# The recurrence's TensorE program written out chunk by chunk, padded to 1280 instructions each, with nine bf16 products ahead of it

## The reference, cut to what matters

```python
def step(carry, xs):
    W_in, W_out = carry
    q_t, k_t, v_t, lr_t = xs
    k_h = softmax(einsum('blhd,bDhd->blhD', k_t, W_in)) * lr_t[..., 1:]
    q_h = softmax(einsum('blhd,bDhd->blhD', q_t, W_in))
    qk = einsum('bqhD,bkhD->bhqk', q_h, k_h) * mask
    o_t = einsum('bqhD,bDhd->bqhd', q_h, W_out) + einsum('bhqk,bkhd->bqhd', qk, v_t)
    W_out = W_out + einsum('bnhD,bnhd->bDhd', k_h, v_t)
    for _ in range(2):
        g_out = -attn(W_in, k_t, v_t)
        g_in = -attn(W_out, v_t, k_t)
        W_in = W_in - lr_in * g_in
        W_out = W_out - lr_out * g_out
    return ((W_in, W_out), o_t)
_, o = lax.scan(step, (W_in0, W_out0), (qc, kc, vc, lrc))
```

## Time and profile before

| what | value |
|---|---|
| median of 3 runs | 2547.16 us |
| the profiled execution's own time | 2548.93 us |
| its span | 2547.1 us |
| TensorE busy | 2187.3 us (86%), 32499 products |
| VectorE, ScalarE, GpSimd busy | 1596.5, 1565.8, 1102.3 us |
| stage B, 434 to 1226 us: mean granted TensorE clock | 0.81 of full |
| stage C, from 1226 us: the same | 0.97 |

### The profile page before, as it was taken

The page is one execution under the profiler, slowest core; times in us unless marked ns, Lnnn a source line. Parts: engine busy times, 40 slices in busy tenths (PEclk is TensorE's granted clock), DMA queues, the critical chain, the costliest instruction groups (busy, mean ns, idle before and its releaser), DMA issues.

```text
span 2547.1 us, 88423 instructions
## 1 busy us (share of the span) xinstructions
PE 2187.3 (86%) x32499; PEld 1393.0 (55%) x32499; DVE 1596.5 (63%) x3901; ACT 1565.8 (61%) x4121; POOL 1102.3 (43%) x1221
## 2 busy tenths in 40 slices
PE   7999995877877777777389999999999999999898
PEld 3555542554544545455246566565665656647466
DVE  6888885665665665666247467474774747647465
ACT  6888873665665665666248456484564846648464
POOL 1221222665666666666523333444233442334323
PEclk9999997787897887878699999999999999999999
DMA  6555556222322323221321231212313122130120
GB/s 203 166 171 156 162 160 163 53 65 64 84 66 65 69 67 78 52 67 38 95 79 42 74 75 43 74 34 74 75 43 87 28 72 69 43 97 4 40 50 18
DMA packets 387244, 201.52 MB, mean 79 GB/s; under 512 B 257376, under 2 KB 372704, under 8 KB 386800
## 3 DMA queue, kind: packets, MB, share of 16 engines
q1 hardware_dynamic: 386800, 195.65, 28.9%
HBM read 101.67 MB, written 69.27 MB: 67 GB/s over the span
## 4 chain that ended last, share of the span: by engine, by line
PE 48%; DVE 16%; issue 15%; ACT 15%; POOL 2%; SPq 2%; DMA 1%; DVEq 1%; ACTq 1%; POOLq 0%
PE psum L1035 11%; ACT arena L1554 8%; DVE arena L1846 6%; PE psum L1128 4%; PE psum L899 4%; PE psum L887 3%; PE psum L894 3%; PE psum L1087 3%; PE psum L1095 3%; ACT arena L1353 3%; PE psum L907 2%; PE psum L1201 2%; PE psum L1067 2%; PE psum L1164 2%; DVE arena L1855 1%
## 5 line engine op out<-in xcount | busy, mean ns | idle before, releaser
L1780 POOL TENSOR_TENSOR arena<-arena 128x400 f32<-128x400 f32 x256 | 218.8, 855 | 483.3 <-DVE arena L2205 483.3
L1353 ACT ACTIVATE arena<-psum,scan_sb 64x128 f32<-64x128 f32 x1152 | 311.5, 362 | 122.4 <-PE psum L964 60.4
L1554 ACT ACTIVATE arena<-psum,arena 128x100 f32<-128x100 f32 x1024 | 271.0, 368 | 6.8 <-DVE arena L2197 6.7
L1846 DVE SCALAR_TENSOR_TENSOR arena<-psum,taps_sb,arena 128x511 f32<-128x511 f32 (+2 forms) x288 | 212.3, 747 | 54.4 <-ACT arena L1253 47.6
L808 PE MATMUL psum<-arena,w_in_sb 128*128 128x512 f32 x512 | 229.7, 597 | 1.0 <-ACT arena L1246 1.0
L1925 DVE TENSOR_TENSOR arena<-psum,scan_sb 64x512 f32<-64x512 f32 x290 | 190.2, 674 | 31.7 <-PE psum L995 18.3
L899 PE MATMUL psum<-arena,scan_sb 128*128 128x512 f32 x264 | 194.7, 829 | 3.8 <-issue 2.0
L894 PE MATMUL psum<-arena 128*32 128x17 f32 x10240 | 140.3, 196 | 64.5 <-issue 39.6
L1596 POOL TENSOR_TENSOR arena<-arena 128x512 f32<-128x512 f32 x64 | 80.8, 1275 | 263.9 <-ACT arena L1279 263.9
L1673 POOL TENSOR_TENSOR arena<-arena 128x512 f32<-128x512 f32 x128 | 133.9, 1068 | 131.7 <-ACT arena L1408 118.6
L2197 DVE TENSOR_REDUCE arena<-psum 128x4 f32<-128x400 f32 x256 | 146.4, 573 | 59.1 <-PE psum L1151 49.1
(11 more groups left out here) (223 smaller groups left out, 4706.9 us busy)
## 6 DMA issues: line engine op xcount, KB each, us to landing
arena<-arena SPq DMA_DIRECT2D x144, 128.0 KB
arena<-x SPq DMA_DIRECT2D x32, 512.0 KB, 3.9
arena<-gates_d SPq DMA_DIRECT2D x112, 128.0 KB, 4.0
v_rows_d<-arena SPq DMA_DIRECT2D x64, 136.0 KB
k_rows_d<-arena SPq DMA_DIRECT2D x64, 136.0 KB
arena<-k_rows_d SPq DMA_DIRECT2D x128, 68.0 KB, 2.0
arena<-v_rows_d SPq DMA_DIRECT2D x128, 68.0 KB, 2.1
v_d<-arena SPq DMA_DIRECT2D x32, 256.0 KB, 4.3
```

The costliest lines, as they stand in the source:

```text
L1353: ins = act.activation(dst.rearrange("p (t x a) -> p t x a", x=PP, a=INNER)[upper, :, x], src.rearrange("p (t a) -> p t a", a=INNER)[upper ...
L1554: act.activation(c_soft[s][:, f % 2, u], sc, ACT.Exp, bias=c_max[s][:, u:u + 1]).then_inc(c_act.mark(f"exp{s}{f}u{u}"), 1)
L1780: pool.tensor_tensor(soft, soft, c_rec[s].unsqueeze(2).broadcast_to([P, 4, KEYS]), ALU.mult).then_inc(c_pool.mark(f"prob{s}{f}"), 1)
L1846: ins = dve.scalar_tensor_tensor(out=a_acc[:, t, j:TOK], in0=bank[2 + t][:, 0:TOK - j], scalar=taps_sb[:, t % KT, col:col + 1], in1=a_acc[ ...
```

## The change

TensorE's loop over rounds becomes a Python loop, so that all 32 chunks stand in its instruction list and all its wait counts are constants. The other engines keep their loops. In each chunk, six `hold` instructions are put behind the transpose `tb1` and ahead of the waits for `pb0`, and one behind `pb1` and ahead of the wait for `wi1`. Ahead of the wait for the start state, nine products of 128x128 by 128x400 in bf16 are put, which write a bank that the later code overwrites.

```diff
             mm.then_inc(st_pe.mark("rates"), 1)
             phase_a_done(pe)
 
+            def keep_busy(count):
+
+                for _ in range(count):
+                    pe.matmul(bank[4][:, 0:2 * KT * KEYS], identb[:], mask_sb[:, 0:2].rearrange("p a b -> p (a b)"), start=True, stop=True)
+
+            keep_busy(9)
             pe.wait_ge(st_dve.sem, st_dve.at(0, "in"))
...
-            with pe.Fori(0, ROUNDS) as n:
+            for n in range(ROUNDS):
...
                     pe.transpose(bank[1][:, 3 * P:4 * P], e_b[:, 1], ident[:]).then_inc(mine.mark("tb1"), 1)
+                    for _ in range(6):
+                        hold(pe)
                     pe.wait_ge(dve.sem, dve.at(c, "xb0"))
...
                     updates(grid(bank[0][:, 0:PP * ROW17], ROW17), pb_in[1], k_rows[i % 2], every).then_inc(mine.mark("pb1"), 1)
+                    hold(pe)
                     pe.wait_ge(dve.sem, dve.at(c, "wi1"))
```

## The result

The changed kernel takes 2502.81 us (median of 4 runs, 2501.26 to 2503.51) against 2547.27 us of the kernel before beside it. The ratio is 0.9821, 95% interval 0.9802 to 0.9840: faster by 1.8%. The forecast was 2453 us; the time lies inside the range of 2415 to 2508 us, but the gain is 44.5 us where 94 us were forecast. In what follows, a chunk is counted from 0 to 31, and "the stop" is TensorE's idle time at the end of a 256-instruction piece of its list.

A forecast was written before the change was run, and what follows sets the result against it. No engine is full: the recurrence is bound by 32 times one chunk's latency, with TensorE stopping at ends of 256-instruction pieces. 792 us becomes 32 x 21.7 + 4 = 698 us, 94 us less, giving 2453 us; range 2415 to 2508 us.

The forecast's parts named there:

- Where the pieces end: TensorE's recurrence: a chunk is 1280 instructions, five pieces of 256, with ends at the same places, one 48 passes into `p2v`.
- The length of the stop: TensorE in `p2v`: one exposed stop of about 1.5 us in each chunk, the other four ends hidden or under 0.9 us.
- my own stretches: Four stretches between `p2v` places in the kernel before: 23.40, 23.31, 21.01, 22.16 us; the two with clocks over 0.9 average 21.6.
- The clock: TensorE in the recurrence: clock lost once a chunk and regained, near 0.9, giving 21.7 us a chunk.
- the clock stays down: Rival, recurrence: one stop in every chunk keeps the clock low all through, 23.4 us a chunk, 2508 us; chance 0.11.
- TensorE's jumps: Head of TensorE's loop, three times: idle time of 1.21 + 3.03 us goes; the chunk period holds no jump.
- only the jumps: Rival, TensorE's loop: other stops merely move idle time that VectorE and ScalarE impose; gain 8 us, 2539 us; chance 0.07.
- The other engines' jumps: Round starts: VectorE 1.3 us late three times, 4 us back, bounds 0 to 8 us; nothing for ScalarE and GpSimd.
- The `hold`s and the nine products: `hold`s ahead of `pb0` and `ti1` cost nothing; nine products take 3.0 us within 6.07 us of TensorE idle time, free.

The follow-up runs named there:

- the three products: Changed kernel with six of its seven `hold`s a chunk, those ahead of `pb0`, replaced by three bf16 products of 128x128 by 128x100: 2480.78 us, ratio 0.9735.
- the scan: TensorE's loop written out against the kernel before, without the nine products and seven `hold`s, 1273 instructions a chunk, so ends drift: 2548.51 us, ratio 1.0003.
- the locked kernel: Changed kernel without the nine products and with `hold`s only from chunk 4 on, so ends drift, then stay in `khv`: 2479.73 us, ratio 0.9706.

## Why the prediction was right and where it failed

*Where the pieces end: right, to the pass.* Ends every 256 instructions, a chunk of 1280, and the first end 16 instructions in. The stop is 48 passes into `p2v` in 28 of 32 chunks, none in `a1`, `b1` or `pb1`. Moving the phase moved the stop by as much (52 passes with 8 instructions, the last pass of `a1` with 16).

*The length of the stop: too small, but that cost nothing.* I took about 1.5 us, between the first chunks of a round (0 to 2.0 us) and the second (1.4 to 2.2 us). It is 2.2 to 2.7 us. The first chunks of a round follow TensorE's own jump, and what they showed doesn't carry over to a chunk in a steady row with the same ends: chunk 0 of the changed kernel, the only one that follows no steady row, has no stop in `p2v` either. The kernel moved by 8 instructions has the ends of those first chunks and the stop of 2.43 us. I also misread my own stretches: each ends just behind the second chunk's stop, so the two that gave 21.6 us held stops of 2.06 and 1.96 us, and the place without a stop, in chunk 16, lies ahead of its stretch. The 21.6 us stood for a stop of 2.0 us and not of 1.5. What decides when the next piece is asked for, once waits stand between two ends, is open: it isn't the number of instructions behind the end (the six `hold`s moved forward changed nothing).

*The clock: this is the step that failed.* The forecast said that with one stop a chunk "should lose the clock once a chunk and get it back, as the third and fourth do", near 0.9. It is 0.81. Where a chunk does have a clock of 0.92, the price was right: eight such chunks take 21.7 us on average, the very number forecast, though their stop is 2.4 us. But they are eight of 31. Seventeen have a clock under 0.80 and take 24.2 us with a stop of the same length. Of the 1.6 us between 21.7 and 23.3 us these seventeen make 1.3, and chunks 0, 8, 16 and 24 the rest; the longer stop makes nothing of it that shows. That the clock is a term by itself, and not only a sign of the stop, the three products show, which took 22 us off with every stop in its place. My rival "the clock stays down", with 23.4 us a chunk and 2508 us, was the right one and had a chance of 0.11. The error was in averaging four stretches and then setting aside the two cold ones as coming from the start and the jump; the unselected mean was 22.5 us, and they were ordinary. Why the clock comes back in one chunk and not in the next, with the same work, place and stop, no run here tells.

*TensorE's jumps: right that they go, wrong that they pay by themselves.* Written out without a fixed phase, the kernel gains nothing (1.0003). The rival "only the jumps" at 2539 us isn't what that gives either: the drifting ends took the 8 us back, by the lengths of its chunks.

*The other engines' jumps: near in size, wrong in the engine.* I charged 4 us to VectorE. TensorE waits 1.4 to 1.9 us three times, which takes the place of the stop; these chunks are 0.8 us longer than the others on average, 2.5 us in all. What it waits for is ScalarE, late by its jump. I had dismissed ScalarE without pricing it.

*The `hold`s and the nine products: free, as forecast.* TensorE's timeline ahead of the recurrence, answering to the earlier trace rows:

```profile
422.17 2.19 PE L878 MATMUL psum<-mask_sb,identb 128*128 128x400 bf16 x9
428.66 0.48 PE L882 MATMUL psum<-ident,arena 128*128 128x128 f32 x1 [4.30 <-DVE arena L1925]
```

They took 2.2 us (not 3.0) inside the wait for VectorE.

*The Trainium skill's rule on crossing blocks* ("Runtime: NRT & Kernel Launch", section "Instruction fetch mechanics") says that a crossing is mostly hidden. That stays contradicted here: a crossing in the middle of `p2v` stops TensorE for 1.4 to 3.0 us, and holding the crossings at one place is worth 1.8% of the kernel, while removing the branches alone is worth nothing measurable. What it says of branches is borne out on ScalarE as well (1.89 us of idle time behind its jump, none when the loop is written out).

## What to carry to other kernels

Where an engine's list is much longer than a piece and runs through dense blocks of short products, look where the pieces end: count instructions between stops in the timeline, and if the distances are multiples of one number, pad the loop body to a multiple of it and choose the phase by a scan, which a body a few instructions short of the multiple gives in a single run. Such a scan shows where a stop is exposed; it doesn't tell the clock of a steady row (chunk 4 had 1.00 and 21.1 us in the scan, and held there a chunk took 22.6 us). Writing out a loop without that is worth nothing here. If two stretches with the same work differ in clock, don't drop the cold ones from the estimate: price the clock by its own term, and spend padding on small products where the engine waits anyway rather than on empty instructions.

## What the runs showed of the hardware that was not expected

- Three bf16 products of 100 columns in a gap of TensorE some 8 us behind the restart raise the mean clock of the recurrence from 0.81 to 0.86 in the changed kernel and take 22 us off. In the locked kernel they take 11 us off by the medians, with intervals that overlap. Directly beside the stop they do next to nothing by the medians.
- An instruction piece of 16 KB takes 0.9 to 1.4 us to fetch, and TensorE restarts 1.1 to 1.6 us after the packet's end (28 stops of the changed kernel). Behind the first product of the piece before, the packet starts after 0.8 us where no wait follows that product before the end (ends 16 instructions earlier), and after 2.5 us where waits do (changed kernel; medians).
- From the first product of `p1v`, behind its waits, to the restart after the next end it takes about 3.9 us in the changed kernel (median of 28 chunks; 3.46 us in chunk 11 above), although the end before it was passed a microsecond earlier; in the kernel with ends 16 instructions earlier it is 697.68 - 694.30 = 3.4 us.
- ScalarE idles 1.5 to 1.9 us behind its loop's jump in the changed kernel, ahead of the table load of 1.28 us that the kernel puts there; with the loop written out the idle time is gone.
